# Sorted top-2 experts in three token groups, with routing, scatters, gathers and norms laid into the neighbouring stages

## The reference, cut to what matters

```python
x1 = _layernorm(x + attn_out, g1, be1)
gate_probs = jax.nn.softmax(x1 @ Wg + bg, axis=-1)            # 8 experts
topk_p, topk_i = jax.lax.top_k(gate_probs, 2)
topk_p = topk_p / jnp.sum(topk_p, axis=-1, keepdims=True)
comb = jnp.sum(jax.nn.one_hot(topk_i, E) * topk_p[..., None], axis=-2)
h = jax.nn.gelu(jnp.einsum('bsd,edf->bsef', x1, W1) + b1, approximate=False)   # f = 512
y = jnp.einsum('bsef,efd->bsed', h, W2) + b2
moe_out = jnp.einsum('bse,bsed->bsd', comb, y)
return _layernorm(x1 + moe_out, g2, be2)
# outside: x = _layernorm(x + that);  x = _layernorm(x + wide attention(x))
```

## Time and profile before

| | |
|---|---|
| median of 3 runs (lowest, highest) | 5848.35 us (5843.68, 5861.05) |
| the profiled execution | 5848.49 us |
| its span in the trace | 5846.5 us |
| busy share of the span: PE, DVE, ACT, POOL | 89%, 69%, 46%, 21% |
| rotary attention in the trace | until 3385.4 us |
| sorted experts | 3385.7 to 3817.5 us |
| wide attention | from 3817.7 us |

### The profile page before, as it was taken

How to read it: one execution, slowest core, us unless ns; L and a number is a source line. 1 busy time by engine, 2 the same in 40 slices (tenths; PEclk the granted TensorE clock), 3 DMA queues, 4 the chain that set the end, 5 groups by cost and what they waited for, 6 DMA issues and landing times. The chain is left out here.

```text
span 5846.5 us, 85273 instructions
## 1 busy us (share of the span) xinstructions
PE 5225.1 (89%) x31156; PEld 2620.0 (45%) x31156; DVE 4051.5 (69%) x7021; ACT 2679.7 (46%) x4489; POOL 1214.1 (21%) x859
## 2 busy tenths in 40 slices
PE   6999997787999999989999928489999999997999
PEld 2333333344567777762222227333433433434676
DVE  7888885774677777769899723677677777763412
ACT  4656665221233333337777805244444444442333
POOL 0110100220122222311210042233334334341000
PEclk7999998787999999999999959799999999998999
DMA  4211110001111111102122022100000000001000
GB/s 87 46 31 30 33 28 11 0 0 57 36 39 26 29 25 29 35 11 39 34 33 36 11 74 65 29 24 12 12 12 16 9 12 16 12 12 37 4 4 8
DMA packets 145923, 155.38 MB, mean 27 GB/s; under 512 B 48612, under 2 KB 92692, under 8 KB 145092
## 3 DMA queue, kind: packets, MB, share of 16 engines
q1 hardware_dynamic: 140904, 140.84, 11.4%
q0 software_dynamic: 4096, 8.40, 0.5%
...
## 5 line engine op out<-in xcount | busy, mean ns | idle before, releaser
L3802 DVE TENSOR_REDUCE wide_max_parts<-wide_p 128x2 f32<-128x1024 f32 x496 | 596.0, 1220 | 139.9 <-PE wide_p L3771 127.4
L732 ACT ACTIVATE attn_w<-l_p 128x512 f32<-128x512 f32 x1024 | 549.3, 597 | 277.6 <-DVE l_p L1176 153.8
L2490 PE MATMUL caus_p<-caus_x_one,big 128*128 128x129 f32 x4608 | 639.9, 286 | 0.0
L583 DVE TENSOR_REDUCE l_max_parts<-l_p 128x2 f32<-128x1024 f32 x512 | 602.1, 1219 | 45.8 <-PE l_p L559 41.4
L2574 ACT ACTIVATE big<-caus_p 128x512 f32<-128x512 f32 (+3 forms) x768 | 344.9, 489 | 573.5 <-PE caus_p L2476 419.4
L2490 PEld LDWEIGHTS caus_p<-caus_x_one,big 128*128 128x128 f32 x4608 | 590.7, 198 | 36.0 <-issue 2.5
L583 DVE TENSOR_REDUCE rot_max_parts<-rot_p 128x2 f32<-128x1024 f32 x488 | 574.2, 1219 | 46.4 <-PE rot_p L559 44.2
L4054 PE MATMUL wide_p<-wide_q,wide_k 64*128 64x512 f32 x2048 | 530.4, 596 | 0.0
L4182 ACT ACTIVATE attn_w<-wide_p 128x1024 f32<-128x1024 f32 x342 | 350.1, 1024 | 356.5 <-PE wide_p L4054 352.9
L3988 POOL TENSOR_TENSOR big<-big,attn_w 128x1024 f32<-128x1024 f32 x128 | 330.1, 2579 | 419.0 <-PE wide_p L3771 407.3
L583 DVE TENSOR_REDUCE caus_max_parts<-caus_p 128x2 f32<-128x1024 f32 (+2 forms) x360 | 340.6, 957 | 24.2 <-PE caus_p L559 15.9
...
## 6 DMA issues: line engine op xcount, KB each, us to landing
...
```

The costliest lines, as they stand in the source:

```text
L583: self.nc.vector.tensor_reduce(self.max_parts[:, 2 * p:2 * p + 2, n, half], pair[:, :, 0:self.width(n, half)], AX.X, ALU.max).then_inc(*se ...
L732: self.nc.scalar.activation(self.exps[t % len(self.exps)], bank, ACT.Exp).then_inc(*self.exped.up())
L2490: mm = nc.tensor.matmul(outs[o % 2][:, nq % 2 * (C + 1):(nq % 2 + 1) * (C + 1)], exps[h % 2][:, kb, nq * P:(nq + 1) * P], x_one[b % 2][:, ...
L3802: self.nc.vector.tensor_reduce(self.max_parts[:, :, n, h], side, AX.X, ALU.max).then_inc(*self.maxed.up())
```

## The change

The expert layer's steps stay the same; where they stand and how tokens are grouped changes.

- `ROUTED = ((0, 16), (16, 8), (24, 8))`: three groups, of batches 0 and 1, of batch 2, and of batch 3. They take 39, 23 and 23 tiles, 85 in 22 quads (before 78 in 20). `Routes` becomes one `Route` a group.
- Route 0 moves into rotary attention. Behind the finish of batch 1 `finish` lays its logits, its 26 pieces on DVE two at a time, its counts, its places, and 32 scatters, one a step. The expert weights (24 ordinary DMAs, into `core.arena`) are issued by SP beside units 13 and 14.
- The expert stage begins with loads of sorted rows. Routes 1 and 2 are laid beside tiles 0 to 29 and 14 to 43, three small DVE steps a tile; their 16 scatters each, and from tile 42 on the 32 gathers of group 0, stand one a tile, and POOL waits before each for the product of that tile (`up_mm`). Behind them come the combines of group 0, the tail of batch 0 alone, and `early`. At the end SP waits for the last store to land.
- The tail of batch 1, and gathers, combines and tails of batches 2 and 3, move into wide attention: 57 steps of `later` there at the start, laid at eight places of each of its first units instead of five (eleven in the first). Their gathers (class `Gathered`, chunks of 2 token tiles, 8 DMAs) land in the space of batch 0's `x_mid`.
- The buffers of the stages share `core.arena` and `core.big` in another way, which adds no instruction.

```diff
+ROUTED = ((0, 16), (16, 8), (24, 8))
 ...
     def finish(u):
         b, g = units[u]
+        if u in (len(units) - 4, len(units) - 3):
+            half = u - len(units) + 4
+            return [[("expert", e)] for e in range((1 - half) * E2 // 2, (2 - half) * E2 // 2)]
         if g < GROUPS - 1:
             return []
 ...
+        if NT * (b + 1) == route.first_tile + route.n:
+            pieces = [("gate_piece",)] * Route.GATES
+            pieces[Route.BEFORE_EXP:Route.BEFORE_EXP] = [("route_exp",)]
+            places = [("place_piece",)] * Route.PLACES
+            steps += [[("logits",)]] + [pieces[i:i + 2] for i in range(0, len(pieces), 2)] + [[("counts",)]]
+            steps += [places[i:i + 2] for i in range(0, len(places), 2)]
+            steps += [[("scatter", s, n)] for n in range(route.n) for s in range(2)]
+        return steps
 ...
-    plan = []
-    for g in range(routes.groups):
-        plan += [("logits", g), ("count", g)] + [("scatter", g, n) for n in range(routes.TILES)]
-    plan += [("load", 0), ("load", 1), ("turn_in", 0), ("weights", 0)]
+    for g, first in ((1, 0), (2, 14)):
+        route = routes[g]
+        pieces = [("gate_piece", g)] * Route.GATES
+        pieces[Route.BEFORE_EXP:Route.BEFORE_EXP] = [("route_exp", g)]
+        lay(first, [("logits", g)] + pieces, 3)
+        lay(first + 9, [("counts", g)])
+        lay(first + 10, [("place_piece", g)] * Route.PLACES, 3)
+        lay(first + 14, [("scatter", g, s, n) for n in range(route.n) for s in range(2)])
+    for c, first in enumerate((3, 7, 11, 15, 33, 37, 49, 53)):
+        lay(first, [("gate_row", c), ("none",), ("biases", c)])
+    done = routes[0].n_out + LAG
+    lay(done + 1, [("gather", c, s, i) for c in range(len(back.chunks)) for s in range(2)
+                   for i in range(back.size)])
+    for c in range(len(back.chunks)):
+        lay(done + 2 * back.size * (c + 1) + 4, [("combine", c)])
+    first = done + 2 * back.size * 2 + 5
+    steps = tail.steps(0)
+    lay(first, steps + [("narrow",)])
+    lay(first + len(steps) + 1, early, 2)
+
+    plan = [("load", 0), ("load", 1), ("turn_in", 0), ("weights", 0)]
 ...
+                elif kind == "gather":
+                    if args == [0, 0, 0]:
+                        pool.wait_ge(*routes[2].owned.at(1))
+                        experts.stored_on(pool, (routes[0].n_out + 3) // 4 - 1)
+                    if new(experts.up_mm, J):
+                        pool.wait_ge(*experts.up_mm.at(J))
+                    back.on_pool(pool, *args)
 ...
-    work, later = [], []
+    work, later = [], tail.steps(1)
+    for b in range(2, nb):
+        chunks = [c for c, (route, at) in enumerate(back.chunks) if (route.first_tile + at) // NT == b]
+        later += [("gather", chunks[0])]
+        for c in chunks:
+            later += [("gather", c + 1)] if c < chunks[-1] else []
+            later += [("none",), ("combine", c)]
+        later += tail.steps(b)
 ...
             else:
                 plan += next_later()
+            if u < PAIRS - 1 and kb in (1, 3, 5):
+                plan += next_later()
```

871 lines of the change are left out of this document (478 added, 393 removed).

## The result

The changed kernel takes **5805.0 us** (median of 4 runs, 5801.3 to 5813.9) against 5847.0 (4 runs, 5843.7 to 5861.1) for the kernel before on the same chip: ratio 0.9926 [0.9906, 0.9946]. It is faster by 42 us, and not by the 137 that I forecast; 5805 lies outside my range of 5672 to 5780. The profiled execution took 5803.1 with a span of 5801.2.

A forecast was written before the change was run, and what follows sets the result against it. PE bounds both attentions; between them it starves beside back-to-back indirect DMAs or idles. Wide attention would begin at 3385.4 + 13 + 6 + 224 + 4 + 4 + 15 = 3651.4, 167 earlier; with +30 there, -137: 5711, range 5672 to 5780.

The forecast's parts named there:

- Start of the expert stage: From the end of rotary attention to the first expert product: 6 us in place of 71.3, a change of -65.
- Tiles, clock, store wait and spaced DMAs: Expert stage: 224 us of tiles and work beside them, +4 half clock, +4 store wait, +15 for 64 spaced indirect DMAs.
- my two fours: Expert stage: +4 us for PE starting at half clock and +4 for SP's wait for the last store.
- Rival A: Expert stage: starvation stays, each of the 64 spaced indirect DMAs costs 0.7 to 1.4 us, 5741 to 5786; chance 0.17.
- rival B: Instruction fetch and DVE's new work are hidden: 0 for the 64 DMAs, 12 in wide, 6 in rotary, 5671; chance 0.13.
- C: All 128 indirect DMAs stand beside work, 32 in each attention; at 1.4 us each 5870, slower than before; chance 0.03.
- D: A link holds the saving back: first load waits for a scatter, or a batch 1 wide projection for its turn, 5736.
- Rotary, +13: Rotary attention grows by 13 us, range 5 to 40, from route 0's logits, its routing on DVE and its scatters.
- three bursts of 12 ... so 3: Rotary attention: scatter bursts would cost 14 us at 0.45 each, but an attention issues fewer, longer instructions, so 3.
- Wide, +30: Wide attention grows by 30 us, range 12 to 70, from the 57 steps moved in.
- 62 x 0.49: Wide attention: about 62 us of added DVE work, each costing 0.49 us as read from batch 0's finish, +30.
- Unit of 48 us with 13 free on DVE: Wide attention: a 48 us unit has DVE 35 in a plain one, 44 after the change, still under PE's.

## Why the prediction was wrong, step by step

- **Start of the expert stage**: right, 6.8 us against 6.
- **Tiles, clock, store wait and spaced DMAs**: right in sum, in part by luck. From the end of rotary to the wide stage I had 6 + 224 + 4 + 4 + 15 = 253, the trace has 262. The 15 for the DMAs was too much (3.5 on the second kind; my 0.25 x 64 is 16 besides), the 224 too little by some 20, an estimate that keeps my two fours, so the two misses partly cancel. Rival A, that spacing by a tile doesn't help, is refuted by the 51 us and the 3.5; rival B is half right, since the spaced DMAs are nearly free, and wrong for DVE's work. C needed 1.2 us for each of 128; the runs showed 51 us for 64 unspaced ones, 0.8 each, and 23 us for the 32 scatters of rotary attention, 0.7 each, both on the first kind; D doesn't appear.
- **Rotary, +13, measured +46**: two terms failed, and the table of rotary's cut at the 340th maximum parts them. The first is "three bursts of 12 ... so 3". I reasoned that an attention with long instructions hardly feels starvation. From the cut on, where the scatters stand, the stage takes 285.3 us for 262.1 before, +23; with spaced scatters or on the second kind it takes 264.0, +2. The rows at 3150 show it: PE is busy 35.8 of 50 us where the second kind has 48.6. The second is "32 logits (3.5 us at full clock)" with 6.5 for DVE's routing. Ahead of the scatters the stage takes 535.7 us for 512.5, +23 where I had 10 (+15 to +25 over the fifteen traces with one row of logits, of either kind). The clock wasn't full there: it fell to 0.64, and with the logits in four steps this part is 10 to 16 us shorter than in the changed kernel. What is left, +7 to +13, is about what I had for logits and routing. On the second kind PE's idle time in rotary grew by 4 us only (35 to 40), its busy time by 23: the waits that routing added for PE came to less than my 6.5. With both put right rotary takes 788.3 and 784.9 us, +14 and +10.
- **Wide, +30, measured +78 (76 on the second kind)**: in the term 62 x 0.49 the 62 failed. It should have been 68 for a start: three tails of 19 and the 32 combines of 0.347 make 68, and so do the traces, 342.3 - 46.0 - 228.2. Above all these were durations from a stage without POOL's additions; beside them the steps, and wide attention's own instructions, took 46 us more, so DVE got 114 us and not 62. The run without thick additions is 41 us shorter. I had seen the rule in the earlier trace rows, but priced it at 8 us, by the smallest of the steps and by one in eight. The trace has two of the eight long, at 4616.75 and 5005.82, each begun just behind an addition of POOL, and in the third meeting the step behind it (L199) took 2.30 us. So all three meetings held a step.

```profile
4616.59 2.36 POOL L3988 TENSOR_TENSOR big<-big,attn_w 128x1024 f32<-128x1024 f32 x1 [2.62 <-PE wide_p L3771]
4616.75 2.24 DVE L195 TENSOR_SCALAR wide_rstd<-wide_std 128x8 int32<-128x8 int32 x1
...
4241.86 2.30 DVE L199 TENSOR_TENSOR wide_square<-wide_rstd 128x8 f32<-128x8 f32 x1
```

  What is left without the held time, 1569.7 - 1532.5 = 37 us for 68, is 0.55 each, so the price of 0.49 was not the fault. By whole units, counted from 0, the trace of before gives about the same: units 9 and 10, where the norms of batch 0 stand, take 48.4 and 46.4 us for 43.6, 7.6 more for 15.3 us more of DVE's busy time, 0.50 each (0.37 by its durations, 20.4). The unit ahead of them must not be counted in: it takes 58.1, but its 14.5 us are 128 products of the output rows on PE (14.7 us), and PE is never idle.

```profile
L249 PE MATMUL wide_p<-big,wide_att 128*128 128x128 f32 x128 | 14.7, 276 | 0.0
```

- **Unit of 48 us with 13 free on DVE**: the 48 was a mean that includes finishes. A plain unit of before takes 43.6 us and DVE is busy 31.7 of it, so 12 are free and the moved 68 us would have fitted into seven units. They didn't hide: 59 us of PE's idle time there end with a maximum, so what counts is when DVE takes the next one. In after, units 0 to 6 take 64.4, 51.0, 56.0, 50.9, 51.0, 58.3 and 50.1 us by the first activation of each, three of them over the "55 or more" that I had named as the sign of a wrong wide term.
- **How the wait looks** in the changed kernel: PE stands 7.3 us for a maximum that DVE took up late, and the clock is at 0.89 to 0.90 in the first stretches where the plain one has 1.00.

```profile
3746.48 3.78 PE L3900 MATMUL wide_p<-x_chn,big 128*128 128x512 f32 x4 [7.26 <-DVE wide_max_parts L3940]
```

- **Range**: rotary and wide both came out beyond their upper ends (40 and 70), and nothing stood against them. I treated the two as independent though both rest on one belief, that DVE's work and POOL's issues mostly fit beside an attention that PE bounds.
- **What one trace could not show**: 77 us of the expert stage before, which the change removes, exist on one kind of chip only. On the other the stage gains 93 us, the two attentions lose 103 in the one pair of traces, and the medians differ by 1.6 us. So that the change gains 42 us at all rests on the kind of chip.

Left open: what differs between the two kinds of chips, and whether it is the chip at all; why bursts of 12 and 16 starve the other engines on the first kind and the bursts of 8 gathers in wide attention don't; what this program would take with spaced scatters, the tail beside tiles and the split logits alone.
